# One cast moved from GpSimd to ScalarE in the attention pipeline of a small language tower, and two splits and two transfers exchanged in order

## The reference, cut to what matters

```python
q  = concat(qn, rope(qr))                        # 16 heads of 96
k1 = concat(kn, rope(kr));  v1 = ckv @ Wv        # branch 1: causal, all keys
ks, vs = 128 selected rows (top_k of a score)    # branch 2: selected keys, rope applied to ks
kw, vw = x @ Wwin_k, x @ Wwin_v                  # branch 3: window of 128 keys, rope applied to kw
o  = g0*attn(q,k1,v1,causal) + g1*attn(q,ks,vs) + g2*attn(q,kw,vw,window)
out = o @ Wproj
```

## Time and profile before

| | us |
|---|---|
| median of 3 runs (lowest to highest) | 1754.34 (1753.4 to 1754.41) |
| the profiled execution | 1754.28 |
| its span | 1752.5 |
| busy in the span: PE, PEld, DVE, ACT, POOL | 1365.7, 1140.4, 1399.5, 1209.9, 1362.3 |

### The profile page before, as it was taken

How to read it: one execution, slowest core, us unless ns; L and a number is a source line. 1 busy time by engine, 2 the same in 40 slices (tenths; PEclk the granted TensorE clock), 3 DMA queues, 4 the chain that set the end, 5 groups by cost and what they waited for, 6 DMA issues and landing times.

```text
span 1752.5 us, 61262 instructions
## 1 busy us (share of the span) xinstructions
PE 1365.7 (78%) x19368; PEld 1140.4 (65%) x19368; DVE 1399.5 (80%) x4989; ACT 1209.9 (69%) x3280; POOL 1362.3 (78%) x1680
## 2 busy tenths in 40 slices
PE   1042388889888988888888888888888888888788
PEld 0021277777777777777777777777777777777643
DVE  4756678888888888878887888878888888888835
ACT  0032178877787788778887788778877887777634
POOL 6775578977897789779987898789877997899510
PEclk9986599999999999999999999999999999999989
DMA  5110133223332323232233233332333332333200
GB/s 99 23 26 6 30 73 54 54 48 69 56 64 48 66 55 61 55 67 55 54 57 63 53 64 55 59 55 54 55 62 52 64 58 42 64 66 69 57 4 22
DMA packets 327657, 93.59 MB, mean 53 GB/s; under 512 B 321104, under 2 KB 323024, under 8 KB 327520
## 3 DMA queue, kind: packets, MB, share of 16 engines
q1 hardware_dynamic: 324448, 88.61, 27.2%
q0 software_dynamic: 3072, 3.15, 1.1%
HBM read 6.64 MB, written 1.05 MB: 4 GB/s over the span
## 4 chain that ended last, share of the span: by engine, by line
POOL 51%; issue 23%; DVE 10%; PE 9%; DMA 3%; POOLq 2%; ACT 2%; DVEq 0%; ACTq 0%; SPq 0%
POOL big L438 9%; POOL big L437 8%; POOL big L398 6%; POOL qk L440 5%; POOL qk L441 5%; POOL vh L492 4%; POOL kparts L469 4%; POOL qparts L458 4%; DVE S L1029 3%; POOL osum L485 2%; PE S L1377 2%; DMA kh<-kparts 2%; POOL o_b L487 2%; DVE big L1039 1%; POOL kparts L472 1%
## 5 line engine op out<-in xcount | busy, mean ns | idle before, releaser
L653 ACT ACTIVATE big<-S,negm 128x128 f32<-128x128 f32 (+3 forms) x1536 | 575.6, 448 | 196.2 <-DVE negm L1029 195.6
L1039 DVE SCALAR_TENSOR_TENSOR big<-PT,big 128x384 f16<-128x384 f32 (+3 forms) x1024 | 471.3, 499 | 17.1 <-ACT big L665 11.4
L665 ACT ACTIVATE big<-PT 128x384 f16<-128x384 f32 (+3 forms) x1024 | 417.3, 458 | 90.1 <-PE PT L1402 67.6
L1029 DVE CUSTOM_DVE_ANT_0 S<-S,mask_c,unscale 128x128 f32<-128x128 f32 (+3 forms) x512 | 284.7, 556 | 160.9 <-PE S L1377 157.3
L1377 PE MATMUL S<-k1T,qh 128*128 128x128 f16 (+3 forms) x1536 | 294.9, 301 | 141.0 <-DMA qh<-qparts 101.3
L1377 PE MATMUL S<-kh,qh 128*128 128x128 f16 (+1 forms) x3072 | 320.0, 241 | 0.0
L1424 PEld LDWEIGHTS O<-vh,big 128*128 128x128 f16 x8064 | 273.7, 96 | 22.9 <-issue 6.3
L1424 PE MATMUL O<-vh,big 128*128 128x33 f16 x8064 | 283.1, 178 | 4.4 <-issue 3.9
L437 POOL TENSOR_TENSOR big<-qk,cst 128x576 f32<-128x576 f32 (+2 forms) x144 | 182.5, 1267 | 104.9 <-ACT qk L594 103.1
L1377 PEld LDWEIGHTS S<-kh,qh 128*128 128x128 f16 x3072 | 227.3, 99 | 55.2
L1409 PE MATMUL PT<-cst,big 128*128 128x128 f32 x1408 | 244.5, 278 | 2.7 <-DVE big L1039 2.6
(11 more groups left out here) (296 smaller groups left out, 2092.0 us busy)
## 6 DMA issues: line engine op xcount, KB each, us to landing
lat_b<-lat_all SPq DMA_DIRECT2D x8, 448.0 KB, 3.1
qh<-qparts SPq DMA_TRANSPOSE x128, 3.1
kh<-kparts SPq DMA_TRANSPOSE x128, 3.5
xnT_all<-xnT_b SPq DMA_DIRECT2D x14, 128.0 KB, 2.5
xn_b<-xn_all SPq DMA_DIRECT2D x8, 128.0 KB, 2.8
xnT_b<-xnT_all SPq DMA_DIRECT2D x8, 128.0 KB, 2.7
out_dram<-h_all SPq DMA_DIRECT2D x8, 128.0 KB, 2.0
xn_all<-xn_b SPq DMA_DIRECT2D x7, 128.0 KB, 2.0
```

Source lines behind the costliest of these rows:

```text
L653: last = nc.scalar.activation(pr[par][:, lo:lo + n], S[par][:, lo:lo + n], ACT.Exp, bias=negm[par][:, k:k + 1], scale=-1.0)
L665: last = nc.scalar.activation(pT[par][:, 0, lo:lo + n], PT[:, lo:lo + n], ACT.Copy, scale=PSCALE)
L1029: last = v.tensor_tensor_reduce(out=z, in0=z, in1=m, scale=unscale[:] if k == 0 else kfix[:], scalar=3.0e38, op0=ALU.add, op1=ALU.min, acc ...
L1039: v.scalar_tensor_tensor(pT[par][:, 1, lo:lo + n], PT[:, lo:lo + n], PSCALE, pT[par][:, 0, lo:lo + n], ALU.mult, ALU.subtract).then_inc(s[ ...
```

## The change

ScalarE makes the keys' high parts in place of GpSimd: a new function `high_key` in turn h, step 2, behind `take_hi` of unit 3 and ahead of `probs` of unit 1 of the next head. `high_values` moves from step 2 (ahead of `take_hi` of unit 3) to step 1 (ahead of `take_hi` of unit 2). GpSimd splits the queries first and then subtracts for the keys' low parts, now behind a wait for ScalarE. SyncE issues the queries' transfer ahead of the keys'. The functions for the first two heads of a row keep their order and their cast on GpSimd.

```diff
                 with sp.Fori(0, NH // 2 - 1) as hp:
                     for par in range(2):
+                        turn_queries(par, b * NH + hp * 2 + (par + 2))
                         turn_keys(par, b * NH + hp * 2 + (par + 2))
-                        turn_queries(par, b * NH + hp * 2 + (par + 2))
...
                 g.tensor_copy(kparts[:, 0, :, NOPE:P], kk[par][:, :, NOPE:P]).then_inc(s["k_high"], 1)
+                low_key(par, b, hh)
+
+            def low_key(par, b, hh):
+                H = b * NH + hh
                 g.wait_ge(s["k_high"], H + 1)
                 g.nop(nofuse=True)
                 g.tensor_tensor(kparts[:, 1, :, NOPE:P], kk[par][:, :, NOPE:P], kparts[:, 0, :, NOPE:P], ALU.subtract).then_inc(s["k_split"], 1)
...
                 rope(qk[par], rt9, cos9, sin9, n)
-                split_key(par, b, hh, n)
                 split_query(par, b, hh, n)
+                low_key(par, b, hh)
...
+            def high_key(par, b, hh):
+                H = b * NH + hh
+                act.wait_ge(s["rope"], b * (NH + 2) + hh + 3)
+                act.wait_ge(s["k_turned"], H * 16 + 16)
+                copy(kparts[:, 0, :, NOPE:P], kk[par][:, :, NOPE:P]).then_inc(s["k_high"], 1)
...
                     if t == 0 and last < 1:
                         evac_q(p, xb + x_index(0, "qp"), H + 1)
-                    if t == 2 and last < 2:
+                    if t == 1 and last < 2:
                         high_values(1 - p, b, h + 1)
...
                     if last < 2 or t < 3:
                         take_hi(u + 1, (t + 1) % NT, U + t + 1, rows)
+                    if t == 2 and last < 1:
+                        high_key(p, b, h + 2)
```

More of the change, by code:

```diff
@@ L347, in _ @@
                     for par in range(2):
+                        turn_queries(par, b * NH + hp * 2 + (par + 2))
                         turn_keys(par, b * NH + hp * 2 + (par + 2))
-                        turn_queries(par, b * NH + hp * 2 + (par + 2))
             turn_first(B - 1)
             for hp in range(NH // 2 - 1):
+                turn_queries(0, (B - 1) * NH + hp * 2 + 2)
                 turn_keys(0, (B - 1) * NH + hp * 2 + 2)
-                turn_queries(0, (B - 1) * NH + hp * 2 + 2)
                 sp.wait_ge(s["xn_row"], hp + 2)
                 sp.dma_start(xn_all[:, hp * NT * C:(hp + 1) * NT * C].rearrange("p (t c) -> p t c", t=NT), xn_b[:]).then_inc(s["xn_kept"], 16)
+                turn_queries(1, (B - 1) * NH + hp * 2 + 3)
                 turn_keys(1, (B - 1) * NH + hp * 2 + 3)
-                turn_queries(1, (B - 1) * NH + hp * 2 + 3)
                 sp.wait_ge(s["rl_psum"], hp + 1)
```

## The result

| | us |
|---|---|
| kernel before, median of 4 runs | 1754.38 |
| changed kernel, median of 4 runs (lowest to highest) | 1771.15 (1770.16 to 1773.32) |
| ratio, 95% interval | 1.0099 (1.0079 to 1.0119) |
| profiled execution, its span | 1770.82, 1769.0 |
| busy: PE, PEld, DVE, ACT, POOL | 1398.9, 1146.3, 1407.9, 1259.1, 1299.4 |

A forecast was written before the change was run, and what follows sets the result against it. The loop through GpSimd and the later transfer binds now; after the change, the one through ScalarE, VectorE and TensorE. Steady pairs +8.4, other turns +0.7, last row -0.8, late transfers -2: +6.3, so 1760.6 us; range 1741 to 1774.

The forecast's parts named there:

- Preparation loop: GpSimd's start through the later transfer to TensorE's restart, then to GpSimd's next start: 20.37 us for two turns, predicted 20.24.
- Which loop wins: Steady turns: two take the larger of 20.24 and 20.7 (ScalarE, VectorE, TensorE without GpSimd), +0.3 over 20.39, +8.4 in 28 pairs.
- The copy, 0.40 a turn: ScalarE's values' copy, now between exponentials and unit 2's high parts, lengthens the loop without GpSimd from 19.93 to 20.73.
- The cast takes 0.56 and the keys' move slips by 0 to 0.16, taken as 0: ScalarE: cast 0.56 us; keys' move out of PSUM 0.16 later, passing 0 to 0.16 a turn to unit 3's scores.
- Nothing stalls on the cast: ScalarE's cast ends about 6.1 us behind GpSimd's start and GpSimd wants it at 6.55, so no stall.
- Late transfers: Five places where the transfer lands late and TensorE stands: each costs 0.4 us less, together -2.
- cast loop: Not in the prediction: TensorE's restart, ScalarE's cast behind TensorE's turns, GpSimd's low key part, keys' transfer, next restart, once per turn.
- The last row: Row with the normalisation, two turns 22.68 us: GpSimd's relief less the copy's cost gives -0.8, bounds 0 and -8.
- Rival 1: GpSimd relief decides: the copy's new place costs nothing, the loop through the last transfer binds; about 1742, chance 0.22.
- Rival 2: TensorE's clock: earlier landing keeps it up at most of five late places, turning +6.3 into about -1; 1753, chance 0.16.
- Rival 3: ScalarE's cast takes 0.98, delaying keys' move, query projection and unit 3's scores: 0.5 a pair, +14, 1775; chance 0.12.

The follow-up runs named there:

- keys-first version: Changed kernel with the values' copy back at step 2 and the old order on GpSimd and SyncE, keys before queries, cast still on ScalarE: 1901.04 us, ratio 1.0825.

## Why the prediction was right in sign and short in size

- **Preparation loop, 20.24.** Nearly right. Last issue 8.19 behind GpSimd's start (predicted 7.95: the queries' issue starts at 6.80, not 6.7, and SyncE starts its second issue 1.39 behind the first, not 1.24), 3.58 to the restart, and 8.57 from restart to start as in the earlier trace rows: 20.34. The order and the cast together gain nothing steady, and the version with the copy back shows just that, at 20.37.
- **Which loop wins.** Right, and shown: with order and cast as they are, the copy's place decides between 1771 and 1750, and TensorE's waits for the transfer fell to 0.89 and 0.94 as was asked.
- **The copy, 0.40 a turn.** 0.30 was measured (1.53 against 1.23), since the copy overlaps its neighbours. VectorE's low parts wait 0.39 and 0.33 for ScalarE, as the prediction asked. It called for 1.63 from the exponentials to the high parts.
- **The cast takes 0.56 and the keys' move slips by 0 to 0.16, taken as 0.** This is the mis-sized term. The row reads 0.61, and in the queue it takes 0.50. Its neighbours were wrong: with the copy gone, the high parts of unit 3 wait 0.25 for TensorE, so the 0.40 is not given back and the move is 0.30 later (0.03 ahead of the maxima of unit 2, against 0.32 in the earlier trace rows). In the turn that opens no pass the leg to unit 3 grows from 2.79 to 3.01 (3.03 in the median of 28), where the prediction passed on nothing; in the other turn it grows by 0.02. The pair is 20.83, not 20.7: 28 x 0.42 = 11.8 against the 8.4 of the sum. The kernel with the copy alone has the leg at 2.79 and the pair at 20.55, and over all kernels the leg goes with the keys' move. No version freed the keys' move in the change without lengthening something else, so the pair of about 20.6 that this would give (an estimate, 20.83 - 0.24) was not seen.
- **Nothing stalls on the cast.** Right in most steady turns: no wait at 834.07. Wrong in late ones, 4.11 at 1181.57.
- **Late transfers, -2.** Wrong in sign. The prediction gave them 0.4 of room and had no cast loop, which passes a late restart on to the next transfer. Two late turns at the ends of rows (12.51 and 12.25) are most of the +4.4 of turn 12 above, and a disturbed pair in the first row (12.66 in place of 11.20) adds 1.5. What makes the first of such transfers late is open; before had late turns at places of its own.
- **The last row, -0.8.** -2.2, inside its bounds. With the copy back it gains 5.3: 144.15 against 149.48. The relief of GpSimd was real there, and the copy ate over half of it.
- **Rival 1 (1742)** describes the kernel with the copy elsewhere better than the change: its condition, a copy that costs nothing, was made true at 1750. **Rival 2**: the wait fell from 1.63 to 0.94 in the steady turns, but late turns kept their price. The prediction set the lower level's price at 1.56 a turn. The turns of the keys-first version nearly agree: 12.57 - 11.11 = 1.46. The Trainium skill ("TensorE: Matmul & The Clock Gate", HAM oscillation) tells of waits for a transfer with slow work behind each. The keys-first version agrees in part: waits of 2.0 in its turns, and a granted clock of 0.50 behind some of them, but not behind each. **Rival 3** gave the way, a late keys' move, at half of its size (0.24 a pair where it had 0.5); its condition, a cast from about 0.7, was too high, since a cast of 0.61 was enough. That the time came out next to its 1775 is luck: the pace of the pairs gives 11.8, and late turns brought most of the rest. The rivals' middles are 1742 and 1775 in their own lines, and 1741 and 1774 in the range.

## What to carry to other kernels

List the loops, not only the busy engines, and for every operation that changes its engine ask what now stands ahead of it there: an in-order queue ties it to all that this queue waits for, and can close a loop that did not exist. A freed engine helps only where its loop binds; first ask which instruction can leave the other loop. A small instruction's price is its place: the same copy of 0.45 costs 0, 7 or 21 us by what it stands between and by which loop binds. And when two loops lie within half a microsecond, a term of 0 to 0.16 that is taken as 0 can be half of the answer. When two transfers gate one consumer, split the wait.

## What the chip showed that I had not expected

- One and the same wait can be followed by full clock or by half clock: the version with the keys first has turns of 11.1 and of 12.6 us, though the waits ahead of both are nearly the same (2.01 at 885.15, with a granted clock of 1.00 all through the turn; 2.02 at 896.24, with 0.50 from 897.83 to 900.90). What decides between them is open. In the nine kernels of this document in which the cast loop does not bind (56 steady turns each), three steady turns show half clock, behind waits of 1.88, 2.19 and 2.25; the longest wait with full clock behind it there is 1.91, and most are 0.9 to 1.6.
- Two transposing transfers issued back to back start 1.38 to 1.39 apart on SyncE although the first shows 1.23 busy; landing takes 3.3 for the queries and 3.4 for the keys (medians), against 3.1 and 3.5 before: together the two are not slower.
